# Attention scores of a two-layer block: the third kind of score unit in pairs under one mask product, the first kind's masks replaced by a Pool instruction on the probabilities, and the router's softmax a third of a step later

## The reference, cut to what matters

```python
x = x + attention(layernorm(x))        # 4 batches, 512 tokens, 128 channels, 16 heads of 8
x = x + experts(layernorm(x))          # 8 experts of width 256, all computed, gate of the best

scores = einsum('bhtd,bhsd->bhts', q, k) / sqrt(8)
scores = scores + slopes[head] * position_of_key
scores = where(causal, scores, -inf)   # key after query: no weight
attn   = softmax(scores)
y      = einsum('bhts,bhsd->bhtd', attn, v)

logits = xf @ gate_w.T + gate_b        # router
logits = logits * rsqrt(mean(logits**2) + eps) * rms_w
gates  = softmax(logits / 0.5)         # the largest gate g; g / (g + 1e-6) scales the experts' sum
```

## Time and profile before

| | us |
|---|---|
| median of 3 runs | 317.31 (317.29 to 317.88) |
| the profiled execution, its own time | 317.27 |
| its span in the profile | 315.5 |
| PE busy | 292.7 (93%) |
| DVE busy | 204.4 (65%) |
| ACT busy | 193.5 (61%) |
| POOL busy | 85.7 (27%) |

### The profile page before, as it was taken

How to read it: one execution, slowest core, us unless ns; L and a number is a source line. 1 busy time by engine, 2 the same in 40 slices (tenths; PEclk the granted TensorE clock), 3 DMA queues, 4 the chain that set the end, 5 groups by cost and what they waited for, 6 DMA issues and landing times.

```text
span 315.5 us, 5489 instructions
## 1 busy us (share of the span) xinstructions
PE 292.7 (93%) x1750; PEld 184.2 (58%) x1751; DVE 204.4 (65%) x817; ACT 193.5 (61%) x323; POOL 85.7 (27%) x213
## 2 busy tenths in 40 slices
PE   7658698999969999999999999999999999999993
PEld 2524355666636666657666666657666665657871
DVE  5528589788877768554777785556776821266871
ACT  6462255557447478758667396857487877535462
POOL 3349411521133065002321172020300501600250
PEclk9795599999999999999999999999999999999999
DMA  6254400130400013002200132002001000000101
GB/s 173 105 150 126 137 2 0 35 124 6 108 12 0 0 38 127 3 0 59 63 3 2 34 89 76 0 21 66 0 6 35 2 2 2 0 0 1 35 0 33
DMA packets 12524, 13.23 MB, mean 42 GB/s; under 512 B 2064, under 2 KB 9104, under 8 KB 12240
## 3 DMA queue, kind: packets, MB, share of 16 engines
q1 hardware_dynamic: 11376, 11.70, 12.0%
q0 software_dynamic: 1024, 1.05, 1.6%
q10 hardware_dynamic: 96, 0.13, 0.2%
HBM read 5.14 MB, written 1.05 MB: 20 GB/s over the span
## 4 chain that ended last, share of the span: by engine, by line
PE 76%; DVE 10%; POOL 4%; DMA 3%; issue 2%; ACT 1%; SPq 1%; DVEq 0%; POOLq 0%; ACTq 0%
PE ffn_bank L861 14%; PE pv_bank L793 11%; PE a_ring L768 11%; PE v_ring L748 11%; PE a_ring L697 5%; PE a_ring L774 5%; PE a_ring L699 4%; PE a_ring L698 4%; DVE unused L1099 4%; DMA q_stack<-q_lo 1%; DMA q_stack<-m_lo 1%; PE v_ring L755 1%; PE v_ring L697 1%; PE v_ring L806 1%; PE v_ring L698 1%
## 5 line engine op out<-in xcount | busy, mean ns | idle before, releaser
L1099 DVE CUSTOM_DVE_ANT_0 unused<-v_ring,cst 128x256 bf16<-128x256 f32 (+3 forms) x256 | 112.2, 487 | 53.1 <-PE v_ring L748 49.3
L571 ACT ACTIVATE probs<-a_ring 128x512 f32<-128x512 f32 (+1 forms) x192 | 91.8, 526 | 62.3 <-PE a_ring L774 61.6
L748 PE MATMUL v_ring<-k_stack,q_stack 128*128 128x512 f32 (+1 forms) x176 | 84.1, 519 | 4.9 <-DMA q_stack<-q_lo 3.3
L768 PE MATMUL a_ring<-q_stack,k_stack 128*128 128x512 f32 (+3 forms) x256 | 73.5, 351 | 2.2 <-DMA q_stack<-m_lo 2.2
L588 ACT ACTIVATE hidden<-a_ring,cols_sb 128x512 f32<-128x512 f32 x64 | 43.4, 689 | 29.5 <-PE a_ring L699 29.2
L768 PEld LDWEIGHTS a_ring<-q_stack,k_stack 128*128 128x128 f32 x256 | 47.5, 195 | 14.9 <-issue 8.7
L861 PE MATMUL ffn_bank<-hidden,w_sb 128*128 128x512 f32 x100 | 51.9, 604 | 0.9 <-ACT hidden L588 0.9
L774 PE MATMUL a_ring<-score_mask,ident_bf 128*128 128x128 bf16 (+1 forms) x192 | 47.7, 250 | 0.0
L748 PEld LDWEIGHTS v_ring<-k_stack,q_stack 128*128 128x128 f32 x176 | 34.6, 205 | 21.6 <-issue 11.4
L793 PE MATMUL pv_bank<-probs,v_ones 128*32 128x256 f32 (+3 forms) x512 | 42.3, 440 | 0.0
L774 PEld LDWEIGHTS a_ring<-score_mask,ident_bf 128*128 128x128 bf16 x192 | 18.6, 97 | 25.4 <-issue 19.9
(11 more groups left out here) (123 smaller groups left out, 346.5 us busy)
## 6 DMA issues: line engine op xcount, KB each, us to landing
q_stack<-q_hi SPq DMA_DIRECT2D x8, 256.0 KB
k_stack<-k_hi SPq DMA_DIRECT2D x60, 32.0 KB
x_in<-x SPq DMA_DIRECT2D x4, 256.0 KB, 3.4
hidden<-w SPq DMA_DIRECT2D x1, 1024.0 KB, 7.5
k_stack<-k_lo POOLq DMA_DIRECT2D x32, 32.0 KB, 2.1
q_stack<-q_lo SPq DMA_DIRECT2D x4, 256.0 KB
w_sb<-w SPq DMA_DIRECT2D x1, 1024.0 KB, 5.1
x_res<-x SPq DMA_DIRECT2D x4, 256.0 KB, 3.1
```

Source lines behind the costliest of these rows:

```text
L571: act.activation(probs[:, n % 2, q, KIND_AT[kind]:KIND_AT[kind] + cols], a_bank()[:, 0:cols], ACT.Exp).then_inc(e_freed, 1)
L748: pe.matmul(dst, q_stack[b % 2][:, s, n * P:(n + 1) * P], k_stack[:, s, quads[0]:quads[-1] + 1, 0:cols], start=True, stop=True).then_inc(v ...
L768: pe.matmul(dst[:, at:at + P * (TB - j)], k_stack[:, s, q, j * P:(j + 1) * P], q_stack[b % 2][:, s, j * P:T], start=(at == 0), stop=False, ...
L1099: ins = dve.tensor_tensor_reduce(unused[:, (uses[0] - 1) % V_BANKS, at:at + cols], bank_[:, at:at + cols], cst[:, C_MASK + T - cols:C_MASK ...
```

## The change

There are four edits.

1. The third kind's units hold two heads each: two matmuls of 256 columns fill one bank, one mask product of 256 columns serves both, and ACT takes one exponential of 512 columns. A step has 10 units for 12. The plans give these two their places.
2. The first kind has no mask product. POOL clears the later keys' weights in `probs` after the exponential (`mask_probs`, one `affine_select` over 4 heads times 128 columns in each step), and PV of the first kind waits for POOL (`probs_masked`) where it waited for ACT.
3. So that an unmasked score cannot overflow too far before it is cleared, one further row of the stacks adds -1e30 for keys 64 to 127 and queries 0 to 63. Its constants come by a further DMA of 128x512 float32 at the start (`corner`), into a part of `probs` that is not yet used.
4. The router's `route` and `gates` stand later, and POOL's list is in another order around the new instruction.

```diff
 EARLY_PLAN = {
-    "exp": (4, 4, 5, 6, 8, 8, 9, 11, 11, 13, 14, 14), "pv": (11, 15), "pv_last": (0,),
+    "exp": (4, 4, 5, 6, 8, 8, 9, 11, 12, 14), "pv": (11, 15), "pv_last": (0,),
 LATER_PLAN = {
-    "exp": (4, 5, 6, 7, 8, 9, 10, 10, 12, 13, 14, 15), "pv": (12, 15), "pv_last": (0,),
+    "exp": (4, 5, 6, 7, 8, 9, 10, 10, 13, 15), "pv": (12, 15), "pv_last": (0,),
 STAGES = {
-    "z_norm": (0, 13, 1), "z": (0, 15, 1), "logits": (2, 4, 1), "route": (2, 13, 1), "gates": (3, 13, 1),
+    "z_norm": (0, 13, 1), "z": (0, 15, 1), "logits": (2, 4, 1), "route": (3, 4, 1), "gates": (3, 15, 1),
 SCALAR_STAGES = {
-    "k_high": (1, 7, -1), "q_high": (1, 11, -1), "gates": (3, 1, 1),
+    "k_high": (1, 7, -1), "q_high": (1, 9, -1), "gates": (3, 6, 1),
...
+    KIND_UNITS = [[(0,), (1,), (2,), (3,)], [(0,), (1,), (2,), (3,)], [(0, 1), (2, 3)]]
+    KIND_END = [4, 8, 10]
...
+            sp.dma_start(corner, consts[:, C_CORNER:]).then_inc(corner_loaded, 16)
             sp.dma_start(cst[:, C_MASK:C_KEY], consts[:, C_MASK:C_KEY]).then_inc(mask_loaded, 16)
...
+            def mask_probs(n):
+                pool.wait_ge(e_freed, UNITS * n + KIND_END[0])
+                triangle = probs[:, n % 2, :, 0:P]
+                pool.affine_select(out=triangle, in_=triangle, compare_op=ALU.is_ge, fill=0.0, base=0,
+                                   pattern=[[0, QUADS], [1, P]], channel_multiplier=-1).then_inc(probs_masked, 1)
...
-                    if s == 0 and b >= 1:
-                        load_k_low(b, 1)
-                        z_rstd(b - 1)
-                    if s == 1 and b + 1 < B:
-                        x_rstd(b + 1)
-                        split_low(b + 1, 0)
-                        split_low(b + 1, 1)
-                    if s == 2 and b + 1 < B:
-                        load_k_low(b + 1, 0)
-                    if s == 2 and b >= 1:
-                        norm_logits(b - 1)
...
+                    if s == 0 and b >= 1:
+                        load_k_low(b, 1)
+                    if s == 1 and b + 1 < B:
+                        x_rstd(b + 1)
+                    if s == 2 and b + 1 < B:
+                        split_low(b + 1, 1)
+                        load_k_low(b + 1, 0)
+                    mask_probs(SETS * b + s)
+                    if s == 2 and b >= 1:
+                        norm_logits(b - 1)
+                    if s == 0 and b >= 1:
+                        z_rstd(b - 1)
+                    if s == 1 and b + 1 < B:
+                        split_low(b + 1, 0)
...
-                act.activation(probs[:, n % 2, q, KIND_AT[kind]:KIND_AT[kind] + cols],
-                               a_bank()[:, 0:cols], ACT.Exp).then_inc(e_freed, 1)
+                act.activation(probs[:, n % 2, quads[0]:quads[-1] + 1, KIND_AT[kind]:KIND_AT[kind] + cols],
+                               a_bank()[:, 0:len(quads) * cols].rearrange("p (q t) -> p q t", t=cols),
+                               ACT.Exp).then_inc(e_freed, 1)
...
+                if kind == 0:
+                    last.then_inc(e_filled, 1)
+                    return
...
-                pe.wait_ge(e_freed, UNITS * n + QUADS * (kind + 1))
+                if kind == 0:
+                    pe.wait_ge(probs_masked, n + 1)
+                else:
+                    pe.wait_ge(e_freed, UNITS * n + KIND_END[kind])
...
+        corner = ROW_Q * q + CONST_TERM
+        c[corner, C_KEY + HALF:C_KEY + P] = MASKED_SCORE
+        c[corner, C_CORNER:C_CORNER + HALF] = 1.0
+        c[alibi + maxima + [corner], C_QUAD + q] = 1.0
```

More of the change, by code:

```diff
@@ L41 @@
 MASKED_SCORE = -1.0e30
+HALF = P // 2
 EPS_LN = 1e-5
@@ L107, in block_kernel @@
     SETS = H // QUADS
-    UNITS = KINDS * QUADS
+    KIND_UNITS = [[(0,), (1,), (2,), (3,)], [(0,), (1,), (2,), (3,)], [(0, 1), (2, 3)]]
+    EXP_UNITS = [(kind, quads) for kind in range(KINDS) for quads in KIND_UNITS[kind]]
+    KIND_END = [4, 8, 10]
+    UNITS = len(EXP_UNITS)
     HB = 6
@@ L562, in a_bank, with exp_unit @@
                 return a_ring[(uses[0] - 1) % A_BANKS]
[L564 removed]
+            def exp_unit(b, s, unit):
                 n = SETS * b + s
[L566 to L568 removed]
+                kind, quads = EXP_UNITS[unit]
+                act.wait_ge(e_filled, UNITS * n + unit + 1)
+                if n >= 2 and unit == 0:
                     act.wait_ge(pv_done, n - 1)
                 cols = 128 * sum(TB - j for j in KEY_BLOCKS[kind])
[L571 to L572 removed]
+                act.activation(probs[:, n % 2, quads[0]:quads[-1] + 1, KIND_AT[kind]:KIND_AT[kind] + cols],
+                               a_bank()[:, 0:len(quads) * cols].rearrange("p (q t) -> p q t", t=cols),
+                               ACT.Exp).then_inc(e_freed, 1)
             def evacuate_pv(b, half):
@@ L628, in _ @@
             k_constants(0)
+            act.wait_ge(corner_loaded, 16)
             q_constants(0)
@@ L652, in _ @@
                     for unit in range(UNITS):
-                        exp_unit(b, s, unit // QUADS, unit % QUADS)
+                        exp_unit(b, s, unit)
                         for stage, of in due(SCALAR_STAGES, b, s, unit, B):
@@ L759, in exp_unit @@
                 n = SETS * b + s
-                kind, q = k // QUADS, k % QUADS
-                if n == 0 and k == 0:
+                kind, quads = EXP_UNITS[k]
+                if n == 0 and kind == 1:
                     pe.wait_ge(mask_ready, 2)
@@ L766, in exp_unit @@
                 at = 0
-                for j in KEY_BLOCKS[kind]:
-                    pe.matmul(dst[:, at:at + P * (TB - j)], k_stack[:, s, q, j * P:(j + 1) * P],
-                              q_stack[b % 2][:, s, j * P:T], start=(at == 0), stop=False, skip_group_check=True)
-                    at += P * (TB - j)
-                blocks = len(KEY_BLOCKS[kind])
-                diagonal = dst[:].rearrange("p (a t) -> p a t", t=P)[:, 0::3, :][:, 0:blocks, :]
+                diagonals = []
+                for q in quads:
+                    for j in KEY_BLOCKS[kind]:
+                        last = pe.matmul(dst[:, at:at + P * (TB - j)], k_stack[:, s, q, j * P:(j + 1) * P],
+                                         q_stack[b % 2][:, s, j * P:T], start=(at == 0), stop=(kind == 0),
+                                         skip_group_check=True)
+                        diagonals.append(at // P)
+                        at += P * (TB - j)
+                if kind == 0:
+                    last.then_inc(e_filled, 1)
+                    return
+                blocks = len(diagonals)
+                step = diagonals[-1]
+                diagonal = dst[:].rearrange("p (a t) -> p a t", t=P)[:, 0::step, :][:, 0:blocks, :]
                 pe.matmul(diagonal, ident_bf[:], score_mask[:].unsqueeze(1).to_broadcast([P, blocks, P]),
```

16 lines of the change are left out of this document (7 added, 9 removed).

## The result

The changed kernel takes 314.42 us (median of 4 runs, 313.67 to 315.2), the kernel before in the same comparison 317.6 (4 runs): a ratio of 0.9901 (0.9872 to 0.993 with 95% confidence; brackets behind a ratio below mean the same). I had said 311.0 us, range 308.6 to 314.4, so the median lies just outside. The sign was right and the size was about half. In all comparisons together two executions, 338.5 us of the kernel before and 359.09 us of the one with the warm start, were in a slower state of the chip, and the ratios leave them out. The profiled execution took 315.2 us, its span is 313.4. That is 2.07 us less than the profiled execution of before, where my sum had 6.25.

A forecast was written before the change was run, and what follows sets the result against it. PE, without a gap from steps 5 to 15 on, was taken to bound the kernel. From 317.27 us, 5.45 (steps 5 to 15), 0.5 (step 0) and 0.3 (steps 1 to 4) came off: 311.0 us, range 308.6 to 314.4.

The forecast's parts named there:

- The price of a mask product: On PE: a small product (128 columns) costs 0.13 us, a large one (256) 0.12; four small ones 0.50 a step.
- The 0.15 for the pairs: Third kind on PE: four products cost 0.39 us a step before, two cost 0.24 after; 0.15 saved.
- Given back at the transposition: Transposition of the maxima waits for DVE, losing 0.15 us in steps 6, 7, 8 and 10 to 14; 1.2 us.
- the gain of 0.65: PE's saving per step in steps 5 to 15: 0.50 first kind, 0.15 third kind; 7.15 us in 11 steps.
- 0.5 for the inverse root: Steps 8 and 12: POOL clears probabilities before the inverse root that z waits for; 0.25 us charged in each.
- The select hidden everywhere: POOL's new instruction, 0.9 us with handovers, hides everywhere before PV of the first kind; room 1.2 us or more.
- rival 4: Slower than before: a long select holds PE at PV of the first kind; at 2.3 us, 321.3 us; chance 0.07.
- rival 5: POOL and DVE hold each other up at SBUF in eight steps; 5.6 us comes back, 316.6 us; chance 0.05.
- Steps 0 to 4: Gain of 0.5 us in step 0 (bounds 0 to 0.9) and 0.3 in steps 1 to 4 (0 to 2.6).
- The router's later softmax at nothing: POOL's normalisation ends about 4 us later in step 6, still before `route` reads it in the next step; no cost.
- My signs of a wrong mechanism: PE idling at PVs, DVE's maxima over 0.3 us after PV (steps 7, 8, 11, 12), or first score unit moving.
- the first: DVE's line takes over in most steps; steps 5 to 15 keep 2.75 us, 0 to 4 0.4; 314.1 us; chance 0.17.

## Why the prediction was right in sign and too large

- **The price of a mask product: right.** 0.50 forecast for four small ones; with the select alone six steps gain 0.50 to 0.54. The 0.15 for the pairs shows in steps 7 and 11 once their first one stands ahead of the PV (0.70 in all against 0.54). In steps 6 and 10 the four are worth less, 0.36 to 0.39, and why is not shown.
- **Given back at the transposition: right**, place and size, 1.26 for 1.2. But the sum took it as a loss within the gain of 0.65. The experiment with pairs only puts it otherwise: it is the whole worth of the pairs.
- **The step that failed** is the sentence that a mask product that goes is worth its whole price in steps 5 to 15, because PE is busy for all of the earlier trace rows's 188.60 us. That row says that PE waits for nobody now, and nothing on how near the next engine is. I asked for that nearness at two handovers, the maxima and the select. For the first kind I forecast 5.0 us (11 x 0.50, less 0.5 for the inverse root), and with the select alone 3.50 came. The copy `yT` holds back 0.34 in each of steps 8 and 12, step 15 brings nothing, and steps 6 and 10 bring 0.25 less together: 1.4 us. For step 15 the chain names ACT behind its table load; no run moved that load, so this cause is read and not tested.
- **The pairs were mis-sized too.** In the sum they are 0.45 us to the good (11 x 0.15, less 1.2). Pairs alone measured 0.45 to the bad in these steps, and the changed kernel gains 0.5 less there than the one with the select only. I had taken 0.04 a step for what the pairs add between the transposition and the last PV; with pairs alone it is 1.14 us in all, 0.37 of it in step 9, where the chain of the changed kernel is DVE's, and 0.04 to 0.10 in each other step. Another 0.1 comes ahead of the first score unit of step 13. Together this is some 0.9 of the 2.5 us missing. Why the small losses arise is not shown.
- **The select hidden everywhere: half wrong.** No PV of the first kind waits for POOL with a price that shows, which was the fear of rival 4. But the select costs 1.24 us: 0.39 in step 1, where it slows `xn`, and 0.40 in each of steps 8 and 12, ahead of POOL's inverse root, where I had charged 0.25. Of rival 5 the mechanism exists, in one step of sixteen and not in eight.
- **Steps 0 to 4.** 0.8 forecast; 0.53 at equal clock (0.66 in step 0, 0.13 lost after it). In the profiled execution the clock rose later and took 1.4 back. That is no step of my sum: I took one execution's clock for the kernel's. Without it the forecast would still have been 2.7 us too low. The added DMA at the start shows no price: the first score unit starts at 36.04 us in one execution of the changed kernel and at 35.32 in the other, against 35.55 before.
- **The router's later softmax at nothing:** the edit shows no price of its own, as I said. But it is not idle: without it the select would cost 3.9 us more in steps 6 and 10.
- **My signs of a wrong mechanism** were too few. PE does not idle at the PVs, DVE's maxima end no more than 0.3 us behind them in steps 7, 8, 11 and 12, and the start did not move beyond what executions differ by. None of the three came, and the time was still 3.4 us above the forecast, because they look only at the handovers that I had already asked about.

Of the rivals, the first was the nearest (314.1): other engines take over in more places than I charged. But it is in four steps (8, 9, 12 and 15) and not in most, and POOL and ACT do it beside DVE. That its number came so close owes something to luck, since 1.4 us of the profiled time are the clock's.

## What to carry to other kernels

That an engine never waits in a stretch does not say how much sooner the others could serve it. Before a saving on it is summed, go through each handover of a period, read when the other engine had finished and when this one began, and cap the saving there. An instruction that nobody waits for can cost at two further places: in an instruction of another engine that runs beside it, and for everything behind it in its engine's list, which also has to wait for what the new instruction waits for. The kernel before with an idle copy of it measures both, and here also caught three falls of the clock that have to be taken out first.

## What the runs showed of the hardware

- The select of 4 x 128 columns took 0.634 us, 128 columns 0.29, so about 0.9 ns a further column, or 0.115 us for each further 128.
- Four f32 scalings on DVE took 1.50 us beside a select on POOL and 1.11 alone; only the first was stretched, from 0.35 to 0.73 us, up to the end of the select.
- Behind 1.65 us of PE's idle time in step 6 the granted clock was 0.50 from 131 to 134 us in one kernel, and behind 1.70 us it was 1.00 in another. Behind the wait for z in step 4 it was 0.50 from 93.4 to 96.4 us in one kernel (1.57 us idle) and 1.00 in the kernel before (1.61). A wait of PE's can so cost twice: 1.92 us in step 6, and 1.57 in step 7 with nothing waiting.
- PE's granted clock rose at two different times in executions of one kernel, worth 1.4 us; more idle products ahead of the first unit brought the full clock before it.
